# The parts of B in four-step rows of 1 KB, with every fourth step turned into one tile by TensorE

## The reference, cut to what matters

```
x_dbl = u @ W_xproj                        # u: (B, L, 256)
dt_r, Bm, Cm = x_dbl[..., :8], x_dbl[..., 8:72], x_dbl[..., 72:]
delta = softplus(dt_r @ W_dt + b_dt)
def step(h, (d_t, B_t, C_t, u_t)):         # for each of the 1024 steps
    dA = exp(d_t[:, :, None] * A)
    h = h * dA + (d_t * u_t)[:, :, None] * B_t[:, None, :]
    y_t = einsum('bdn,bn->bd', h, C_t)
```

## Time and profile before

| | |
|---|---|
| median of three runs | 2208.34 us |
| the profiled execution's own time | 2209.82 us |
| its span, first to last instruction | 2208.2 us |
| TensorE busy | 2133.7 us (97%) |
| VectorE busy | 1833.8 us (83%) |
| ScalarE busy | 1617.4 us (73%) |
| GpSimd busy | 926.1 us (42%) |
| first scan starts | 163.44 us |

### The profile page before, as it was taken

One profiled execution on the slowest core, in us unless ns is written; L12 is line 12 of the kernel. 1 busy time (PEld: TensorE's weight loads), 2 busy tenths in 40 slices (PEclk: granted clock), 3 DMA queues, 4 the chain that ended last, 5 costly groups with the idle time before them and its releaser, 6 DMA issues.

```text
span 2208.2 us, 50669 instructions
## 1 busy us (share of the span) xinstructions
PE 2133.7 (97%) x17080; PEld 1270.6 (58%) x17080; DVE 1833.8 (83%) x2721; ACT 1617.4 (73%) x2160; POOL 926.1 (42%) x453
## 2 busy tenths in 40 slices
PE   7978999999999999999999998999999999999998
PEld 3432333333333333333333336899999999999997
DVE  6879999999999999999999997666565556556775
ACT  5878999999999999999999995445455455545453
POOL 3124344444444444444444333544444444444542
PEclk9978999999999999999999999999999999999999
DMA  5994212121212122222222134000100010000000
GB/s 172 299 281 133 49 41 48 40 48 40 48 40 47 40 47 42 45 44 44 45 42 46 41 86 149 1 0 0 39 1 0 0 39 1 0 1 2 14 10 15
DMA packets 354957, 114.93 MB, mean 52 GB/s; under 512 B 283000, under 2 KB 345600, under 8 KB 354624
## 3 DMA queue, kind: packets, MB, share of 16 engines
q1 hardware_dynamic: 350416, 110.92, 20.0%
q10 hardware_dynamic: 4464, 3.02, 0.4%
HBM read 67.98 MB, written 45.88 MB: 52 GB/s over the span
## 4 chain that ended last, share of the span: by engine, by line
PE 41%; DVE 29%; issue 23%; SPq 3%; ACT 2%; POOL 1%; DVEq 1%; DMA 0%; ACTq 0%; POOLq 0%
DVE arena L1588 25%; PE PS L1364 20%; PE PS L1352 16%; PE PS L1249 1%; ACT behind L981 1%; SPq L519 1%; SPq L615 1%; SPq L521 1%; PE PS L1232 1%; ACT behind L971 1%; PE PS L1331 1%; PE PS L1219 1%; PE PS L1340 1%; DVE arena L1431 0%; PE PS L1142 0%
## 5 line engine op out<-in xcount | busy, mean ns | idle before, releaser
L1588 DVE TENSOR_TENSOR_SCAN arena<-behind 128x1040 f32<-128x1040 f32 x512 | 1153.8, 2308 | 14.3 <-ACT behind L981 10.6
L1109 ACT ACTIVATE arena<-PS,arena 128x512 f32<-128x512 f32 x512 | 344.6, 688 | 405.8 <-PE PS L1352 405.3
L971 ACT ACTIVATE behind<-PS 128x1024 f32<-128x1024 f32 x512 | 526.4, 1028 | 100.7 <-DVE arena L1588 52.5
L1249 PE MATMUL PS<-arena 128*32 128x128 f32 x8192 | 566.2, 406 | 0.0
L981 ACT ACTIVATE behind<-PS 128x1024 f32<-128x1024 f32 x512 | 540.0, 1055 | 16.4 <-PE PS L1232 9.4
L1364 PEld LDWEIGHTS PS<-arena 128*128 128x128 f32 x4096 | 473.2, 192 | 7.7
L1364 PE MATMUL PS<-arena 128*128 128x128 f32 x4096 | 473.5, 275 | 0.0
L791 POOL COPY behind<-carry 128x64 f32<-128x64 f32 x128 | 212.9, 1664 | 508.2 <-ACT carry L998 266.8
L1249 PEld LDWEIGHTS PS<-arena 128*32 128x32 f32 x8192 | 234.9, 119 | 287.5 <-issue 211.3
L1352 PE MATMUL PS<-parts_xh,parts_w 128*128 128x512 f32 x1536 | 383.4, 401 | 9.5 <-ACT arena L1109 6.5
L1736 DVE SCALAR_TENSOR_TENSOR arena<-PS,arena 128x128 f32 (+1 forms) x508 | 142.8, 343 | 258.3 <-PE PS L1364 257.2
(11 more groups left out here) (139 smaller groups left out, 1433.4 us busy)
## 6 DMA issues: line engine op xcount, KB each, us to landing
dl_d<-arena SPq DMA_DIRECT2D x48, 256.0 KB, 3.5
du_d<-arena SPq DMA_DIRECT2D x48, 256.0 KB, 3.5
arena<-dl_d SPq DMA_DIRECT2D x512, 24.0 KB
arena<-b_d SPq DMA_DIRECT2D x64, 192.0 KB
arena<-du_d SPq DMA_DIRECT2D x512, 24.0 KB
b_d<-arena SPq DMA_DIRECT2D x48, 128.0 KB, 2.4
u_d<-behind SPq DMA_DIRECT2D x8, 512.0 KB, 3.9
sz_d<-arena SPq DMA_DIRECT2D x8, 512.0 KB, 4.7
```

What stands on the lines that cost most here:

```text
L971: nc.scalar.activation(seg(dA[:, half])[:, :, 1:], PS[:, 0:2, :].rearrange("p j (i t) -> p (j i) t", t=TC), ACT.Exp).then_inc(exp_done, 1)
L1109: nc.scalar.activation(hT[:, e % 2, c], PS[:, HIDDEN[(GT * e + c) % 3], :], ACT.Gelu, bias=bias1[:, lp, e * GT + c:e * GT + c + 1]).then_i ...
L1249: last = nc.tensor.matmul(PS[32 * j:32 * j + 32, 4 + kk, 0:DB], cd[:, pair, j, 32 * i:32 * i + 32], seg(hb[kk])[:, :, 1 + 16 * j + i], sta ...
L1588: nc.vector.tensor_tensor_scan(hb[kk][:, q * QD * SEG:(q + 1) * QD * SEG], dA[:, q % 2], dB[:, G_, lo:lo + QD * SEG], 0.0, ALU.mult, ALU.a ...
```

## The change

In `b_d` four steps of one row now lie side by side: the tensor is indexed by half (the lower or upper four steps of eight), group of eight steps, sequence, pair, step within four, state. For this the step of a partition changes: TensorE takes as its stationary operand every fourth column of u (a stride of four fp32 numbers, 16 B) and not 128 neighbours, so that partition p of tile t holds step 4p + t, and the four tiles of one partition are four neighbouring steps. A store then moves 1 KB a row from one partition. There are still six stores an item: for each half (every second partition) one for each part, which repeats its source over the three, two or one pairs that use it. For those to be neighbours, `W_PART` and `X_PART` are exchanged. On the load side Bst comes in two loads of 48 rows instead of one of 96, and its rows are ordered half, sequence, pair, step within four; the eight loads of rhs_u write 12 partitions four apart instead of 12 neighbours. The bytes of every tensor stay as they were.

```diff
-W_PART = (0, 1, 2, 0, 1, 0)
-X_PART = (0, 0, 0, 1, 1, 2)
+W_PART = (0, 0, 0, 1, 1, 2)
+X_PART = (0, 1, 2, 0, 1, 0)
+HALF = ROWS // 2
-    b_d = nc.dram_tensor("b_d", (NIT, TT, 2, PAIRS, 2 * N), bf16).ap()
+    b_d = nc.dram_tensor("b_d", (NIT, 2, TT // OCT, 2, PAIRS, OCT // 2, 2 * N), bf16).ap()
-        DU_LOADS = 16 * (OCT + 1)
+        DU_LOADS = 16 * (OCT + 2)
@@ load_products
-                sp.dma_start(Bst[kk][0:ROWS], b_d[it].rearrange("(o e) b p n -> (e b p) o n", e=OCT)
-                             [:, bass.ds(o, NOCT), :]).then_inc(du_in[kk], 16)
+                for half in range(2):
+                    sp.dma_start(Bst[kk][half * HALF:(half + 1) * HALF], b_d[it].rearrange("h o b p k n -> h (b p k) o n")
+                                 [half, :, bass.ds(o, NOCT), :]).then_inc(du_in[kk], 16)
                 for e in range(OCT):
-                    sp.dma_start(rhs_u[kk][RW * e:RW * e + RW, :, e, :], src[e, kk, :, bass.ds(o, NOCT), :]
+                    sp.dma_start(rhs_u[kk][e // 4 * HALF + e % 4:(e // 4 + 1) * HALF:4, :, e, :], src[e, kk, :, bass.ds(o, NOCT), :]
@@ the stores of B, item k
-                for p in range(PAIRS):
-                    sp.dma_start(b_d[it, :, bb, p, :].rearrange("(k p) n -> p k n", p=P),
-                                 b_part[bb][W_PART[p]].rearrange("p k b n -> p k (b n)")).then_inc(a_rows[bb], 16)
+                for half in range(2):
+                    for w in range(PARTS):
+                        rows = [p for p in range(PAIRS) if W_PART[p] == w]
+                        src = b_part[bb][w][half:P:2].rearrange("o k b n -> o (k b n)")
+                        sp.dma_start(b_d[it, half, :, bb, rows[0]:rows[-1] + 1].rearrange("o r k n -> o r (k n)"),
+                                     src.unsqueeze(1).broadcast_to([P // 2, len(rows), 4 * 2 * N])
+                                     ).then_inc(a_rows[bb], 16)
@@ TensorE, B of item k
-                                                u_s[bb][:, h, t * P:(t + 1) * P], wx_s[:, h, N + R:],
+                                                u_s[bb][:, h, t:TT:4], wx_s[:, h, N + R:],
```

## The result

| | before | after |
|---|---|---|
| median | 2209.11 us (2207.08 to 2210.83) | 2221.7 us (2219.72 to 2223.56) |
| ratio, 95% interval | | 1.0059 [1.0047, 1.0071] |
| profiled execution, its span | 2209.82, 2208.2 us | 2220.9, 2219.1 us |
| first scan, last scan start | 163.44, 1334.62 us | 173.94, 1347.05 us |

The direction was right. The size was not: 12.6 us between the medians where the forecast had 4.0, outside the range given.

The account below looks back on a forecast made before the run. The first scan's start was taken to bound the kernel: strided weight loads make item 7 9.0 us late, against a 5.0 us prize from SP's lag, so 2208.3 + 4.0 = 2212.3 us, range 2202.5 to 2214.

Parts of the forecast that it names:

- The place: Front: the first scan's start decides, through SP and ScalarE's first exponential; the loop takes over any shift in full.
- The weight load at 0.215 us: TensorE's block for B: each strided weight load takes 0.215 us instead of 0.109, adding 1.7 us an item.
- A: TensorE's strided read is free, first copy 5.0 us earlier, 2203.3 us; chance 0.30.
- B: TensorE's strided weight load costs half the price, 0.16 us; kernel 2.4 us faster, 2206 us; chance 0.12.
- D: TensorE's strided weight load costs four times the price, 33 us late less 5.0, 2236 us; chance 0.03.
- 9.0 us late at item 7: Front's end: seven items at 1.7 us, 11.9 less usable slack, make item 7's silu 9.0 us late.
- The 12 partitions four apart carry the same packets: SP's eight loads of rhs_u: stepped partitions cost nothing, 0.3 us either way.
- sets the first copy: ScalarE's first exponential, ending at 159.6 us, fixes the first copy at 159.7 instead of 155.75, +4.0 us.
- SP is no longer late: Front's end: item 6's B ready at about 146, SP's loads start at about 150 and land by 157.
- Stores in 3.0 us: SP issues an item's six B stores in 3.0 us instead of 3.94; lower bound nothing gained.
- Rival C: B's stores get no cheaper and the stride is free; 0 to 1 us gained, 2207.8 us; chance 0.05.
- The sum: First copy 155.75 to 159.7, +4.0 us, shifting the loop with it; 2212.3 us.

Follow-up runs that it names:

- e1: The kernel before with only TensorE's stationary operand for B reading every fourth column of u: 2216.78 against 2210.03 us, ratio 1.0032.
- e6: The changed kernel with rhs_u written to 12 neighbouring partitions again, stride, stores and two Bst loads kept: 2216.59 us, ratio 1.0033 to the kernel before.
- e2: The kernel before with only the load side changed, Bst in two loads and rhs_u to partitions four apart: 2215.24 us, ratio 1.0026.
- e4: The changed kernel with TensorE reading 128 neighbouring columns of u again: 2216.34 us, ratio 1.0031 to the kernel before.
- e11: The changed kernel with neighbouring columns for TensorE and neighbouring partitions for rhs_u, layout and two Bst loads kept: 2210.29 against 2209.69 us, ratio 1.0003.
- e3: The kernel before with only the store side changed, 1 KB rows in the new order, W_PART and X_PART exchanged: 2210.22 us, ratio 1.000.
- e7: The changed kernel with rhs_u's 12 partitions two apart instead of four: 2220.07 us, timed once.
- e8: The changed kernel with rhs_u's 12 partitions eight apart over all 96 rows: 2219.03 us, timed once.

## Why the prediction was wrong, point by point

- **The place: right in the main.** The start of the first scan makes 10.5 of the 12.4 us, the loop takes a shift over in full, and what decides is the race of SP against ScalarE's first exponential. The prediction did not have the second place, block 1's wait for the front's last stores: 1.9 us.
- **The weight load at 0.215 us: right in kind, a little small.** It is 0.229 (3.67/16), close to the 0.234 of line 1249's row, which had been used as the upper bound. An item costs 1.93 and not 1.7 us. Rivals A, B and D fall with it.
- **9.0 us late at item 7: too small.** Line 1185 starts there at 148.15, 12.5 later than line 1179 at 135.66. Seven items at 1.93 are 13.5, less 3.6 of slack 9.9. Some 1.7 us more come from the granted clock. From 118 to 121 us it is 0.50, the level of 1.2 GHz, with TensorE busy throughout, and line 1148 takes 8.83 us there and not 7.14. After has two such rows, the kernel before and e1 have one. That makes part of this step chance: with one, e1's exponential is 11.3 late; with two, after's is 12.6. Of what is left, 1.4 and 1.0, the stretch ahead of item 0's B makes 0.8 and 0.4 (it starts at 34.77 in e1 and 34.32 after, 33.96 before). Another 0.35 is slack that could not be used: line 1185 starts 1.77 us behind line 1157 and not 1.72, seven times.
- **The step that failed: "The 12 partitions four apart carry the same packets: nothing, 0.3 us either way."** The packets are the same; the issue isn't. Eight loads take 6.70 us of SP and not 4.50, or 3.50 where only their step is undone (e6), and stand on the path once at block 0. That is why the exponential no longer "sets the first copy": from the first load of B to the matmul it takes 165.12 - 154.70 = 10.4 us, 7.2 before. e2 measures 0.26% for it together with Bst in two, after against e6 and e4 against e11 0.26 and 0.28% for the step alone. The same issue again for block 1 delays the last stores of the front to 195.97, and block 1's scan waits for them, another 1.9 us.
- **"SP is no longer late": wrong in the outcome.** SP did lose its lag at item 6's stores (they start when their data is ready). But the data were forecast ready at 146 (by the prediction's own terms, 7 x 1.7 less 3.4 of slack, it should have been 147.3) and came at 149.58, issue took 3.91 and not 3.0, and the loads started at 154.70 and not at 150.
- **Stores in 3.0 us: wrong.** They take 3.91, as in the lower bound of that part (nothing). It is even a little worse: SP came to them from a wait, and e1's old stores, also behind a wait, take 3.25. Rival C's half about the stores was right; e3 finds 1.000. The DMA engines' share fell as worked out, and no wait was ended by it.
- **The sum.** Stride 0.32%, stepped loads 0.26%, layout nothing: 0.58% against 0.59% measured. In the profile the same adds up along SP's path: the stores of item 6 start 149.60 - 142.29 = 7.3 us later, from the first load of B to the first copy it takes 3.2 us more (166.25 - 154.70 against 155.75 - 147.44), and block 1's wait adds 1.9, 12.4 in all. The forecast had 4.0 us where the stride alone (e1) cost 6.8, and for the loads nothing. The direction was right for the reason given, since the stride alone makes the kernel slower; the part left out points the same way.
- **Slips that changed nothing.** The two full slices of the earlier trace rows reach from 55 to 166 us, not to 110. In rival B 16 x 0.05 is 0.8 and not 0.85.

## What to carry to other kernels

A queue that issues DMAs is an engine like the others: on a path that runs through it, price the change by the duration of each issue. Here that duration followed the pattern of partitions and not the bytes or the count of rows. A layout that makes packets larger gains only where something waits for the transfer; here nothing did, and its side effects put time on two engines that had none to spare, TensorE and SP. Putting six stores in another place gained 0.12%, where the larger packets alone gained nothing. Where a weight load of TensorE has to read with a stride, two fp32 numbers apart was nearly free and four cost double.

Follow a late queue to the end of its list too: what it issues last can hold a wait that lies a block further on.

## What the runs showed of the hardware that was not expected

- SP's issue of a load into 12 partitions is 304 ns in the median for neighbours and 792 ns for partitions 2, 4 or 8 apart, with the same packets (e6, e7, after, e8).
- A store from every second partition issues in 0.61 us whether it has 64, 128 or 192 rows of 1 KB, not less than one of 512 rows of 256 B from all partitions (0.54, median of line 615 before).
- Weight loads of 128 fp32 columns: 0.109, 0.114, 0.172 and 0.229 us at stride 1, 2, 3 and 4. ScalarE's strided read had shown 425 against 392 ns; it was no guide for TensorE here.
